# Wide attentions: the value products of two head pairs issued together in every second tick, with a third buffer of transposed exps

## The reference, cut to what matters

```python
h = _layernorm(x, axis=-1) * (1 + ca) + sa
x = x + ga * attention(h)
# inside, layer 0 (causal, RMS norm and rotation of q and k) and layer 1 (bias by distance, not causal)
scores = jnp.einsum('bhqd,bhkd->bhqk', q, k) * scale + bias      # layer 1; layer 0 has a causal mask instead
attn = jax.nn.softmax(scores, axis=-1)
a = jnp.einsum('bhqk,bhkd->bhqd', attn, v)
return a.reshape(B, S, N_HEAD * HEAD_DIM) @ o_w.T
```

## Time and profile before

| what | us |
|---|---|
| median of 3 runs (lowest, highest) | 3086.98 (3078.37, 3092.64) |
| the profiled execution's own time | 3088.29 |
| its span in the trace | 3086.4 |
| layer 0's wide attention (75 to 697) | 622 |
| layer 1's wide attention (1083 to 1690) | 607 |
| TensorE matmul busy, whole span | 2810.8 (91%) |

### The profile page before, as it was taken

The page is one execution under the profiler, slowest core; times in us unless marked ns, Lnnn a source line. Parts: engine busy times, 40 slices in busy tenths (PEclk is TensorE's granted clock), DMA queues, the critical chain, the costliest instruction groups (busy, mean ns, idle before and its releaser), DMA issues.

```text
span 3086.4 us, 68911 instructions
## 1 busy us (share of the span) xinstructions
PE 2810.8 (91%) x25404; PEld 1877.8 (61%) x25404; DVE 2170.7 (70%) x5846; ACT 1696.3 (55%) x4083; POOL 1049.0 (34%) x1444
## 2 busy tenths in 40 slices
PE   5999999989999999999998889999989979998885
PEld 2666666666666666666665455577666655555663
DVE  5888888855666566666665788556677777786557
ACT  2877787773333377777775566543345543334553
POOL 5877877731000011111112454222332311014313
PEclk8999999999999999999999999999989989899997
DMA  3011111123000001111112544000144431245630
GB/s 102 15 29 29 29 29 29 29 70 97 15 1 1 20 15 29 29 34 32 31 34 74 157 131 130 16 1 15 42 144 138 120 96 35 61 93 159 186 113 28
DMA packets 189836, 188.13 MB, mean 61 GB/s; under 512 B 14288, under 2 KB 166032, under 8 KB 188736
## 3 DMA queue, kind: packets, MB, share of 16 engines
q1 hardware_dynamic: 189504, 183.73, 22.7%
HBM read 130.36 MB, written 53.31 MB: 60 GB/s over the span
## 4 chain that ended last, share of the span: by engine, by line
PE 62%; DVE 21%; issue 6%; ACT 6%; POOL 2%; DMA 2%; SPq 2%; DVEq 0%; ACTq 0%; POOLq 0%
PE pb L174 56%; ACT big L902 4%; PE pb L627 2%; DVE big L2123 2%; DVE big L792 2%; DVE big L245 1%; SPq L1804 1%; ACT big L171 1%; DVE big L775 1%; DVE big L703 1%; DVE big L2612 1%; DVE big L190 1%; PE pb L560 1%; DVE big L774 1%; PE pb L2094 1%
## 5 line engine op out<-in xcount | busy, mean ns | idle before, releaser
L174 PE MATMUL pb<-big 128*128 128x128 f32 (+13 forms) x20220 | 2533.0, 332 | 165.2 <-DVE big L2123 57.6
L174 PEld LDWEIGHTS pb<-big 128*128 128x128 f32 (+5 forms) x20220 | 1571.6, 146 | 923.5 <-issue 546.4
L171 ACT ACTIVATE big<-pb 128x512 f32<-128x512 f32 (+7 forms) x1444 | 826.4, 619 | 598.6 <-PE pb L174 346.7
L171 ACT ACTIVATE big<-pb,big 128x512 f32<-128x512 f32 (+2 forms) x520 | 312.0, 624 | 641.7 <-PE pb L174 518.4
L2123 DVE TENSOR_REDUCE big<-pb 128x4 f32<-128x1024 f32 (+1 forms) x256 | 278.2, 1087 | 111.0 <-PE pb L174 107.6
L185 POOL TENSOR_TENSOR big<-big 128x128 f32<-128x128 f32 x224 | 98.9, 457 | 688.6 <-DVE big L182 688.6
L902 ACT ACTIVATE big<-big 128x256 f32<-128x256 f32 x512 | 253.9, 497 | 69.2 <-DVE big L797 67.3
L902 ACT ACTIVATE big<-pb,big 128x128 f32<-128x128 f32 (+1 forms) x512 | 255.6, 513 | 64.8 <-DVE big L777 64.4
L981 POOL TENSOR_TENSOR big<-big 128x512 f32<-128x512 f32 x128 | 159.7, 1274 | 248.5 <-DMA big<-recip 248.5
L792 DVE CUSTOM_DVE_ANT_0 big<-pb,big 128x256 f32<-128x256 f32 x512 | 186.6, 421 | 80.0 <-PE pb L174 79.9
L1478 DVE SCALAR_TENSOR_TENSOR big<-pb,big 128x128 f32<-128x128 f32 x512 | 143.9, 344 | 139.1 <-PE pb L174 138.5
(11 more groups left out here) (136 smaller groups left out, 2318.5 us busy)
## 6 DMA issues: line engine op xcount, KB each, us to landing
big<-parts SPq DMA_DIRECT2D x96, 512.0 KB, 4.2
parts<-big SPq DMA_DIRECT2D x384, 96.0 KB, 2.3
big<-recip SPq DMA_DIRECT2D x64, 512.0 KB, 6.8
big<-comb SPq DMA_DIRECT2D x32, 512.0 KB, 8.4
parts<-big SPq DMA_DIRECT2D x192, 64.0 KB, 2.1
big<-gates SPq DMA_DIRECT2D x8, 1024.0 KB, 6.0
big<-in_wa SPq DMA_DIRECT2D x2, 2048.0 KB, 9.1
big<-in_wf SPq DMA_DIRECT2D x1, 3072.0 KB, 14.9
```

Source lines behind the costliest of these rows:

```text
L171: return e.activation(o, i, f, bias=bias, scale=scale)
L174: return e.matmul(o, l, r_, start=start, stop=stop, skip_group_check=True)
```

## The change

TensorE no longer does V(t - 2) in every tick: in odd ticks from 3 on it does V(t - 3) and V(t - 2) one behind the other, and in even ticks none. TS gets a third buffer, so that a pair's copies wait for V(p - 3). The buffer is WM in layer 0, and in layer 1 the last 256 columns of WF with WM. As WM is now taken during layer 1's wide attention, SyncE loads WM and CT for layer 2 later, in the narrow attention behind it, at its element 5. The third projection of values moves from tick 4 to tick 5, on TensorE and with it on VectorE, which copies it out. VectorE waits at the very end of each wide attention for all values.

```diff
@@ program
         WF = alloc(6400)
+        spare_at = top[0] - 256
         WM = alloc(768)
@@ wide_attention
-            TS = [alloc(2 * width) for _ in range(2)]
+            TS = [alloc(2 * width) for _ in range(2)] + [WM if causal else big[:, spare_at:spare_at + 1024]]
...
-            v_at = (2, 3, 4, 7)
+            v_at = (2, 3, 5, 7)
@@ turned_out, value
-                return (TS[p % 2].rearrange("p (n q) -> p n q", n=n)[:, :, 64 * half:64 * half + 64],
+                return (TS[p % 3].rearrange("p (n q) -> p n q", n=n)[:, :, 64 * half:64 * half + 64],
...
-                               TS[p % 2][:, width * i + 256 * kb:width * i + 256 * kb + 256 - q0], kb == 0, kb == 1)
+                               TS[p % 3][:, width * i + 256 * kb:width * i + 256 * kb + 256 - q0], kb == 0, kb == 1)
@@ tensor
-                    if 0 <= t - 2 < 128:
+                    if t >= 3 and t % 2:
+                        value(e, t - 3)
                         value(e, t - 2)
@@ ts_writable
-                if p >= 2:
-                    e.wait_ge(pair_valued, p0 + p - 1)
+                if p >= 3:
+                    e.wait_ge(pair_valued, p0 + p - 2)
@@ vector, behind the loop
+                e.wait_ge(pair_valued, p0 + 128)
@@ sync of wide_attention
-                    e.dma_start(CT, dr["c2"]).then_inc(ld_wm, 16)
-                    e.dma_start(WM, dr["wmod2"]).then_inc(ld_wm, 16)
@@ sync of the narrow attention
                     if k == 1 and b == 5:
                         tail.sync(e)
+                        e.dma_start(CT, dr["c2"]).then_inc(ld_wm, 16)
+                        e.dma_start(WM, dr["wmod2"]).then_inc(ld_wm, 16)
```

## The result

| what | before | after |
|---|---|---|
| median of the runs (lowest, highest), us | 3086.98 (3078.37, 3092.64) | 3109.75 (3105.88, 3111.80) |
| the profiled execution's own time, us | 3088.29 | 3111.80 |
| its span, us | 3086.4 | 3109.9 |
| layer 0, first to last record of the wide scores, us | 609.6 | 624.8 |
| layer 1, the same, us | 600.4 | 609.0 |

The changed kernel takes 1.0073 of the time before (95% interval 1.0060 to 1.0086): slower by 23 us, or 0.7%. The last three rows divide the span: up to the first wide scores 78.3 and 77.2 us, between the two attentions 395.3 and 393.9, behind them 1402.7 and 1405.0. All of the difference lies in the two wide attentions, +15.1 and +8.5 us.

What follows compares the result with a forecast made beforehand. TensorE was taken to bound both wide attentions, with lost cover outweighing the saving: +10 us in layer 1, +15 in layer 0, -1.5 for first and last groups, +23.5 in sum, giving 3111 us, range 3092 to 3127.

Steps and rivals of the forecast that it cites:

- the first and last groups: Groups of eight ticks at the ends of the wide attentions: -0.3 us each for five, -1.5 us.
- The saving: Both wide attentions, TensorE: a pair of ticks saves 0.15 us, 19 us in all if nothing else moves.
- Tick 1: The reciprocals' transposes hang on tick 0's scores, so V's cover becomes wait: +0.95 us per group in layer 1, +0.80 in layer 0.
- Tick 7 in layer 0: Output projection c1 waits for a bank ScalarE reads behind the exps; that chain doesn't hold V: +0.80 us per group.
- Tick 3: T(2) waits for the exps: +0.62 us per group in layer 1 (scores' 0.03 included), +0.3 to 0.45 in layer 0.
- T(3) and tick 5: Per group: layer 0 T(3) 0.15 to 0.5 us, tick 5 -0.6; layer 1 tick 5 +0.15 or -0.6 by group.
- At nothing: Third TS buffer, later loads of CT and WM, and VectorE's last wait were to cost no time.
- the cover holds: Rival, both wide attentions: new waits stay short and only the saving is left, -19 us, 3069; chance 0.08.
- the move pays for layer 0: Rival: moving the third projection makes layer 0 even, layer 1 gains every second group: +5, 3092; chance 0.20 with results nearby.
- VectorE becomes the bound in layer 0: Rival: VectorE's lateness goes through ticks 3 to 5 to the exps, +40 us or more, 3128; chance 0.08.

Runs made afterwards that it cites:

- run 9: Kernel before with the third buffer and later loads, V paired in tick 1 of each eight only: 3118.74 us, ratio 1.0103.
- run 4: Changed kernel with the reciprocals' transposes one tick later, at the head of tick 2: 3113.31 us, ratio 1.0090.
- run 6: Changed kernel with the output projection c1 ahead of the values' projection in tick 7: 3099.98 us, ratio 1.0039.
- run 7: Kernel before with the output projection c1 ahead of the values' projection in tick 7: 3075.99 us, ratio 0.9962.
- run 10: Kernel before with the third buffer and later loads, V paired in tick 7 of each eight only: 3083.50 us, ratio 0.9986.
- run 2: Kernel before with only the third projection of values moved from tick 4 to tick 5: 3087.57 us, ratio 1.0009.
- run 12: Kernel before with the fourth projection of values in tick 5 instead of 7, values single, two buffers: 3057.92 us, ratio 0.9908.
- run 1: Changed kernel with single V in every tick and the third projection back in tick 4; buffer, later loads and last wait stay: 3085.80 us, ratio 1.0002.
- run 3: Changed kernel with the third projection of values back at tick 4, V still paired: 3137.23 us, ratio 1.0170.
- run 5: Kernel before with the reciprocals' transposes one tick later, at the head of tick 2: 3099.44 us, ratio 1.0035.
- run 8: Kernel before with both edits, reciprocals' transposes at the head of tick 2 and output projection first in tick 7: 3088.26 us, ratio 1.0000.

## Why the prediction was right

**The time.** 3111 was forecast and 3109.75 measured; 15 + 10 - 1.5 us stood against +15.1 and +8.5. That the total agrees to 1 us is partly **luck**: layer 1's full groups gave +12.4 us for +10, layer 0's +14.6 with a clock fall of 1.4 us in it that no term had, and the first and last groups -3.4 in all for -1.5, most of it from the one tick shown above, which was not foreseen. The mechanism also holds term by term, in layer 1 throughout. The terms below are the differences of the columns, less the V that left or came.

**The saving** of 0.15 us per pair of ticks is in the rows: 1.88 us for two V where two apart cost 2.04, and no way out of V in the even tick. In layer 0 the second V lengthens columns 0 and 2 by 0.65 each, for 0.66. The Trainium skill (TensorEngine Tiling (Array Packing), Key Properties) gives a cause, that a change of tiling mode drains TensorE; the trace agrees, at about 0.15 us for each V that no longer stands alone, though its rows show the time and not the drain. By that rule alone the time would have been 3069, and the runs say 3110: the rule fits and is the small term.

**Tick 1.** Layer 1: the column keeps 4.24 although 1.02 us of V left, and the small wait in column 0 (0.08) went: 0.95, as costed. Layer 0: 4.16 and 5.19 unchanged with 0.81 gone, for 0.80. Run 9 has it by itself; run 4 shows that the chain of maxima, copy and exps stands directly behind it, so that only 0.13 to 0.47 us of the wait can be given away.

**Tick 7 in layer 0.** 7.51 and 7.95 unchanged with 0.81 gone, for 0.80. Runs 6, 7 and 10 confirm it, run 7 also that it costs real time.

**Tick 3.** Layer 1: T(2) was to wait 0.54 and the scores 0.03. Column 4 should be 3.71, a tick without projection or wait, plus the second V, 0.87, and it is 5.12: 0.54 of wait. Column 3 is 3.51 where 4.49 - 1.02 gives 3.47. In layer 0 the term was **mis-sized**: column 4 is 4.47 where 3.65 + 0.66 gives 4.31, so T(2) waits 0.16 and not 0.35.

**T(3) and tick 5.** Layer 1: a column 5 without waits is 3.71 + 0.78 - 1.02 = 3.47 (0.78 is the projection, 4.49 - 3.71), a column 6 is 5.42 + 0.87 = 6.29 (5.42 is what it has in runs 2 and 12, without waits). In 3.79 and 6.60 are then 0.32 + 0.31 = 0.63 of waits, for 0.54 + 0.59 = 1.13 before (4.25 - 3.71 and 6.01 - 5.42): -0.50 (forecast -0.6) in kind A. In kind B 0.04 + 0.59 are left of 0.25 + 0.14: +0.24 (forecast +0.15). In layer 0 the forecast was one number for both kinds, T(3) +0.35 and tick 5 -0.6, together -0.25, and here the two kinds part. Without waits column 5 is 3.65 + 0.86 - 0.81 = 3.70 (0.86 is the projection there, 4.51 - 3.65) and column 6 is 5.61 + 0.66 = 6.27 (5.61 from run 12). By these kind A has 0.08 us of waits left of 0.86, which is -0.78; kind B has 0.91 + 0.63 = 1.54 where it had 1.10, which is +0.44. With tick 1, tick 7, the 0.16 of tick 3 and the saving, the sums are +0.39 and +1.62 per group, mean 1.0 for the 1.1 forecast: **two errors of opposite sign that nearly cancel**. The alternation of the groups, which I used in layer 1, holds for layer 0 too, and there I averaged it away.

**At nothing** were the buffer, the moved loads and VectorE's last wait: run 1, to within 0.1%.

**The rivals.** That the cover holds (3069) fell with tick 1 alone. That the move pays for layer 0 (3092) has its mechanism: by runs 2 and 3 the move is worth 27 us once the pairs are there (in the profiles some 2 us of them are clock falls) and nothing without them, but tick 1 and tick 7 stand outside its reach. That VectorE becomes the bound in layer 0 did not come: it is busy for 493 of 637 us, and light columns of 3.7 us pass without a wait.

## What to carry to other kernels

Work that fills a wait is not free to move. Before grouping it, list for each tick the chains that start at a fixed point (here: scores to maxima to reciprocals, and scores to exps to squares to a bank), and ask how much of the moved work lies under each. If none of the chain holds the work, the whole of it turns into a wait, here 0.8 to 1.0 us against a saving of 0.15.

A wait that one removes by moving its victim can uncover the next chain from the same start (run 4), and can shift a third engine's work on top of another's (run 5, read from the rows); a wait for a buffer in a ring is better removed by the order in which the ring is taken (runs 7 and 12). And a schedule is judged as a whole: the move of a projection was worth 0, 27 or 29 us, depending on the place it went to and on what else stood there. And before a difference of a few us between two profiles is explained, look at the parts that the edit doesn't touch: here they differed by up to 12 us.

## What the runs showed of the hardware that was not expected

**A wait of 2.2 us was followed by 3.4 us at half the clock.** In run 9 TensorE waits 2.24 us for the reciprocals in tick 1 of the kind B groups of layer 0, six times, until 113, 195, 278, 360, 442 and 524 us. TensorE in such a place:

```profile
359.53 0.38 PE L569 MATMUL pb<-big 128*32 128x128 f32 x1 [2.24 <-DVE big L741]
359.71 1.92 PE L175 MATMUL pb<-big 128*128 128x512 f32 x2
361.41 1.06 PE L561 MATMUL pb<-big 128*128 128x128 f32 x4
```

and the windows view of the same stretch, granted clock third from the right:

```profile
359.50:360.50 1.00, 0.97 (x2) 0.52 (x3) 1.00 (x3) 1.00 (x5) 1.00 (x1) 0.55 0.00 0
360.50:361.50 1.00, 1.00 (x3) 0.31 (x2) 0.16 (x1) 0.82 (x4) 1.00 (x2) 0.50 0.00 1
361.50:362.50 1.00, 1.00 (x7) 0.67 (x7) 0.74 (x2) 0.00 (x0) 1.00 (x2) 0.50 0.06 16
362.50:363.40 0.90, 0.90 (x12) 0.81 (x14) 0.55 (x1) 0.89 (x2) 0.40 (x2) 0.72 0.00 0
```

The clock is at 0.50, that is 1.2 GHz in place of 2.4, until about 363 us. L561 with its four transposes takes 1.06 us where the changed kernel has 0.60, and the tick is 1.6 us longer. The changed kernel has the same waits of 2.26 us there and fell once, run 3 three times, run 6 four times; the kernel before, with 1.4 us there, never. In layer 1 the clock fell in full groups twice each in runs 2 and 5 and four times in run 8, behind waits for L839 of 1.5 to 2.3 us, and once in layer 0 in run 4, behind waits of 1.21 and 0.60 us. So a wait can cost more than its own length, and how often a group meets the fall differs between kernels with the same wait; why, was not settled.

**A short VectorE instruction under GpSimd's scalings lasts several times its usual.** L797 on 128x4 takes 1.06 us at 1321.09 and 0.17 at 1326.33, behind the scalings, and the norm's two L245 take 1.31 us before and 2.33 in run 5, in the rows shown there; in a group without scalings over them (1399.88 us before) they take 0.59. By the Trainium skill (SBUF — State Buffer, Who interferes with whom) GpSimd and VectorE share a port pair; a VectorE instruction of the kind `tensor_scalar`, as these are, can need it, and then whichever of the two issues first holds it for its whole instruction while the other is blocked. The trace agrees: each of the four scalings lasts 4.96 / 4 = 1.24 us, and the stretched instructions took about that at most (2.33 / 2 = 1.17). L797 ends at 1322.15, with the second scaling (1319.62 + 2 x 1.24 = 1322.10). In the trace a blocked instruction looks busy, not waiting.
